# Windowed attention and expert layer: attention by halves of a unit, and a new end of the attention part

## The reference, cut to what matters

```python
def ref(x, w_qkv, w_out, wg, w1, b1, w2, b2):          # x: 4 x 1024 x 256, fp32
    xn = layernorm(x)
    return x + attn(xn, w_qkv, w_out) + ffn(xn, wg, w1, b1, w2, b2)

def attn(x, w_qkv, w_out):                             # 16 heads of 16, blocks of 64 tokens
    q, k, v = split(x @ w_qkv)
    # each block of 64 queries sees its own 64 keys and those of the block before,
    # of these the last 64 up to and with the query itself
    scores = einsum("bhnqd,bhnkd->bhnqk", q_blocks, [k_before, k_own]) / 4
    attn = softmax(where(band_mask, scores, -1e30))
    ob = einsum("bhnqk,bhnkd->bhnqd", attn, [v_before, v_own])
    return ob.reshape(B, L, 256) @ w_out

def ffn(x, ...):       # 8 experts, each token to its best 2, capacity K*N/E, hidden 1024
    ...                # out = sum of gate * y[expert, slot]
```

## Time and profile before

| | |
|---|---|
| median of three runs | 739.16 us (738.99 to 740.17) |
| the profiled execution | 741.44 us |
| its span, first to last instruction | 739.6 us |
| mean granted clock of TensorE | 0.963 |
| PE busy | 687.7 us, 93% |
| DVE busy | 448.9 us, 61% |
| ACT busy | 451.2 us, 61% |
| POOL busy | 379.7 us, 51% |
| the chain that ended last | PE 34% of the span, DVE 2%, issue 1% |

### The profile page before, as it was taken

One profiled execution on the slowest core, in us unless ns is written; L12 is line 12 of the kernel. 1 busy time (PEld: TensorE's weight loads), 2 busy tenths in 40 slices (PEclk: granted clock), 3 DMA queues, 4 the chain that ended last, 5 costly groups with the idle time before them and its releaser, 6 DMA issues. The chain is left out here.

```text
span 739.6 us, 19999 instructions
## 1 busy us (share of the span) xinstructions
PE 687.7 (93%) x6841; PEld 602.1 (81%) x6841; DVE 448.9 (61%) x1679; ACT 451.2 (61%) x1457; POOL 379.7 (51%) x542
## 2 busy tenths in 40 slices
PE   5663899999999999999999998999999999999994
PEld 3453689898898998989989897888888988888874
DVE  7983343543435435344353432798989898998992
ACT  4642570934808438074390741798888888887980
POOL 4646460543605435145251401668666859498772
PEclk9866799999999999999999999899999999999998
DMA  9734131142311422224222003241535343443421
GB/s 306 267 112 146 35 111 55 64 142 85 102 61 64 142 85 89 69 69 135 92 83 73 16 22 106 71 128 53 142 107 156 100 129 105 125 118 97 128 87 67
DMA packets 59224, 76.58 MB, mean 104 GB/s; under 512 B 9488, under 2 KB 51728, under 8 KB 59152
## 3 DMA queue, kind: packets, MB, share of 16 engines
q1 hardware_dynamic: 52656, 58.83, 25.3%
q0 software_dynamic: 6144, 16.79, 7.9%
q10 hardware_dynamic: 352, 0.04, 0.0%
HBM read 51.95 MB, written 17.04 MB: 93 GB/s over the span
## 5 line engine op out<-in xcount | busy, mean ns | idle before, releaser
L1091 ACT ACTIVATE a_p<-a_p,a_nmax 128x128 f32<-128x128 f32 x512 | 198.0, 390 | 34.3 <-DVE a_nmax L1125 33.4
L750 DVE TENSOR_TENSOR m_hl<-m_hf,m_hh 128x512 fp32r<-128x512 f32 x128 | 93.3, 729 | 99.9 <-ACT m_hh L707 99.9
L66 PE MATMUL m_psY<-m_w2h,m_hh 128*128 128x256 f32 x512 | 145.0, 283 | 0.0
L66 PE MATMUL m_psY<-m_w2l,m_hh 128*128 128x256 f32 x512 | 143.9, 281 | 0.0
L66 PE MATMUL m_psY<-m_w2h,m_hl 128*128 128x256 f32 x512 | 143.8, 281 | 0.0
L703 ACT ACTIVATE m_hf<-m_psF,b1T 128x512 f32<-128x512 f32 x128 | 88.3, 690 | 66.2 <-PE m_psF L66 52.0
L1125 DVE CUSTOM_DVE_ANT_0 a_p<-a_psS,mask 128x128 f32<-128x128 f32 x512 | 117.5, 286 | 14.0 <-issue 8.6
L671 POOL CAST m_w2h<-raw 128x256 fp32r<-128x256 f32 x64 | 26.0, 407 | 178.1 <-PE m_psY L66 120.5
L66 PE MATMUL m_psF<-m_xh,w1h 128*128 128x512 f32 x256 | 103.5, 404 | 1.9 <-DVE m_xl L727 1.9
L66 PE MATMUL m_psF<-m_xl,w1h 128*128 128x512 f32 x256 | 102.0, 398 | 0.0
L66 PE MATMUL m_psF<-m_xh,w1l 128*128 128x512 f32 x256 | 102.0, 398 | 0.0
(11 more groups left out here) (193 smaller groups left out, 1364.7 us busy)
## 6 DMA issues: line engine op xcount, KB each, us to landing
raw<-in_L_ffn_w SPq DMA_DIRECT2D x16, 1024.0 KB, 5.5
y_scratch<-y SPq DMA_DIRECT2D x64, 128.0 KB, 1.7
n_xin<-in_L_attn_x SPq DMA_DIRECT2D x8, 512.0 KB, 7.8
xn_scratch<-n_xn SPq DMA_DIRECT2D x8, 512.0 KB, 7.1
a_res<-in_L_attn_x SPq DMA_DIRECT2D x8, 512.0 KB, 4.4
a_rall<-recip_scratch SPq DMA_DIRECT2D x32, 128.0 KB
out<-a_res SPq DMA_DIRECT2D x8, 512.0 KB, 4.3
xnr<-xn_scratch SPq DMA_DIRECT2D x7, 512.0 KB, 5.5
```

The source lines that it names most:

```text
L66: last = pe.matmul(out, a, b, start=(n_start and i == 0), stop=(n_stop and i == n - 1))
L750: dve.tensor_tensor(hl[:, u // HC, u % HC, :], hf[:, u % FR, :], hh[:, u // HC, u % HC, :].bitcast(fp32), ALU.subtract).then_inc(hl_done, 1)
L1091: act.activation(e, e, ACT.Exp, scale=-1.0, bias=nmax[:, r, j:j + 1], accum_out=sums[:, r, j:j + 1]).then_inc(exp_done, 1)
```

## The change

Seven edits, all in the attention phase:

- The second and third group of a unit change places: first both sets of heads for the first four blocks (tiles 0 and 1), then both for the last four. `mt` and `half`, `o_cols`, the band of the mask and the waits of "o" on `o_low` follow.
- On DVE four kinds of waits are left out, each implied by another wait of the same engine: `t_done` before maxima, `rr_in` before the transpose of reciprocals, `pv_done` before the copy to `pT`, and `acc` before the adds of tiles 1 to 3.
- The reciprocals of the last group don't go through DRAM. DVE copies them, each repeated 16 times, into `wide`, which POOL has cleared at the start of the phase (64 partitions by 256 numbers, twice). PE multiplies `wide` by `fold` (two identity matrices added, made at the start by DVE), in four fp32 matmuls of 64 columns into `psR`, a part of a bank of the scores. ACT copies the result to `rall`.
- ACT, and not DVE, copies the transposes of step 126.
- Behind step 127 each engine's work is written out. PE: transposes of step 125, values of group 30, transposes of step 126, the product of tile 0, transposes of step 127, the spreading, the product of tile 1, values of group 31. DVE: copy of step 124, reciprocals, the two copies to `wide`, copy of step 125, multiply of group 30, the last add of unit 6, copy of step 127, adds of tiles 0 and 1, multiply of group 31, adds of tiles 2 and 3.
- The products of tiles 2 and 3 go by halves of the sum: the first halves of both wait for `o_low` of group 30, the second halves for that of group 31.
- The last unit is stored tile by tile, 128 KB each, as soon as each is added.

```diff
         def o_cols(parts, n):
             w, i = n // (STEPS // GRP), n % (STEPS // GRP)
-            return parts[w % 2][:, i // 2, (i % 2) * BLK * WIN:(i % 2 + 1) * BLK * WIN]
+            return parts[w % 2][:, i % 2, (i // 2) * BLK * WIN:(i // 2 + 1) * BLK * WIN]
...
             store(UNITS - 2)
-            spread(GROUPS - 1)
-            store(UNITS - 1)
+            for i in range(O_FIRST, NI):
+                j = ITEMS[i][1]
+                sp.wait_ge(item_free[i % 2], count[UNITS, i] + 1)
+                sp.dma_start(ov[:, LAST_U * UT + j:LAST_U * UT + j + 1, :], res[LAST_U % 2][:, j:j + 1, :])\
+                    .then_inc(res_out[LAST_U % 2], 16)
...
             pool.memset(pad_cols(va[1]), 0.0).then_inc(pads, 1)
+            pool.memset(wide[:, :, :], 0.0).then_inc(zeroed, 1)
...
+            g = ALL - 2
+            act.wait_ge(t_done, g + 1)
+            act.activation(pT[:, g % PTR, :, :].rearrange("p c q -> p (c q)"), psP[g % 2][:, :], ACT.Copy).then_inc(pT_last, 1)
+            act.wait_ge(o_full, LAST_G - 1)
+            act.wait_ge(wide_out, 1)
+            act.activation(rall[LAST_G % 2][:, :], psR[:, :], ACT.Copy).then_inc(rall_last, 1)
...
-                dve.wait_ge(acc, w * K * UT)
+                if j == 0:
+                    dve.wait_ge(acc, w * K * UT)
...
-                    if t >= PR:
-                        dve.wait_ge(t_done, t - PR + 1)
                     alone(dve, s_done, t + 1)
...
-                    if n >= 2:
-                        dve.wait_ge(rr_in[half], 64 * (n // 2))
                     dve.transpose(rrow[half][:, :], rsum[:, :]).then_inc(row_out, 1)
...
                     dve.wait_ge(t_done, g + 1)
-                    if g >= PTR:
-                        dve.wait_ge(pv_done, (g - PTR) // GRP + 1)
...
+            dve.tensor_tensor(fold[:, :], m.eye[:, 0:WIN], m.eye[:, WIN:P], ALU.add).then_inc(fold_done, 1)
...
+            copy(ALL - 4)
+            reciprocals(LAST_G)
+
+            dve.wait_ge(zeroed, 1)
+            for s in range(2):
+                rows = slice(s * WIN, (s + 1) * WIN)
+                each = rsum[rows, LAST_G % 2 * GRP * BLK:(LAST_G % 2 + 1) * GRP * BLK].rearrange("p (c j) -> p j c", j=BLK)
+                dve.tensor_copy(wide[rows, :, :].rearrange("p j (c s d) -> p j c s d", s=2, d=DH)[:, :, :, s, :],
+                                each.unsqueeze(3).broadcast_to([WIN, BLK, GRP, DH])).then_inc(wide_done, 1)
+            copy(ALL - 3)
+            multiply(LAST_G - 1)
+            for w, i, kind, j in ended(ALL):
+                read_item(w, i, kind, j)
+            copy(ALL - 1)
+            for i in range(O_FIRST, O_FIRST + UT // 2):
+                add_out(UNITS, i, ITEMS[i][1])
+            multiply(LAST_G)
+            for i in range(O_FIRST + UT // 2, NI):
                 add_out(UNITS, i, ITEMS[i][1])
...
-                if begins and kind == "o" and j == 0:
-                    pe.wait_ge(o_low, w * (STEPS // GRP))
+                if kind == "o" and (groups or begins and j % (UT // 2) == 0):
+                    pe.wait_ge(o_low, groups or (w - 1) * (STEPS // GRP) + 2 * (j // (UT // 2) + 1))
...
-                mt, half = s // (2 * GRP), s // GRP % 2
+                half, mt = s // (2 * GRP), s // GRP % 2
...
-            for i in range(O_FIRST, O_FIRST + UT):
-                product(UNITS, i, range(3 * KD))
+            turn(ALL - 3)
+            values(LAST_G - 1)
+            turn(ALL - 2)
+            product(UNITS, O_FIRST, range(3 * KD))
+            turn(ALL - 1)
+
+            pe.wait_ge(fold_done, 1)
+            pe.wait_ge(wide_done, 2)
+            for j in range(BLK):
+                ins = pe.matmul(psR[:, j * WIN:(j + 1) * WIN], wide[:, j, :], fold[:, :], start=True, stop=True)
+            ins.then_inc(wide_out, 1)
+            product(UNITS, O_FIRST + 1, range(3 * KD))
+            values(LAST_G)
+            for k in range(KD):
+                for i in range(O_FIRST + UT // 2, NI):
+                    product(UNITS, i, range(3 * k, 3 * k + 3), GROUPS - KD + 1 + k)
```

More of the change, by code:

```diff
@@ L828, in attention_phase @@
     GROUPS = ALL // GRP
+    LAST_U, LAST_G = UNITS - 1, GROUPS - 1
     LAG_I, LAG_Q, LAG_RS, LAG_T, LAG_C, LAG_V, LAG_M, LAG_H = 1, 2, 2, 3, 4, 5, 8, 9
@@ L885, in attention_phase @@
         rall = [sb(f"a_rall{i}", [P, BLK * WIN], fp32) for i in range(2)]
+        wide = sb("a_wide", [P, BLK, P], fp32)
+        fold = sb("a_fold", [P, WIN], fp32)
         pT = sb("a_pT", [P, PTR, BLK, P], fp32)
@@ L894, in attention_phase @@
         bank_of = (0, 1, 0, 2)
+        psR = psS[1][:, 0:BLK * WIN]
         psP = [ps("a_psP0"), ps("a_psP1")]
@@ L908, in attention_phase @@
         q_done = sem("a_q_done")
+        zeroed, fold_done, wide_done, wide_out, pT_last, rall_last = (sem(f"a_{n}") for n in
+            ("zeroed", "fold", "wide", "wide_out", "pT_last", "rall_last"))
         pv_done = sem("a_pv_done")
@@ L997, in _ @@
             store(UNITS - 2)
-            spread(GROUPS - 1)
-            store(UNITS - 1)
+            for i in range(O_FIRST, NI):
[3 more added lines that the diff above has]
+                    .then_inc(res_out[LAST_U % 2], 16)
             for u in range(2):
-                sp.wait_ge(res_out[u], 16 * B)
+                sp.wait_ge(res_out[u], 16 * (B - 1 + (UT if u == LAST_U % 2 else 1)))
         @block.gpsimd
@@ L1081, in read_item @@
                                    ACT.Copy).then_inc(item_free[bank], 1)
-            for t in range(ALL + LAST):
+            for t in range(ALL):
                 for w, i, kind, j in ended(t):
                     read_item(w, i, kind, j)
[L1086 to L1092, removed]
+                r = t % PR
+                for j in range(BLK):
+                    act.wait_ge(max_done, t * BLK + j + 1)
+                    e = pr[:, r, j, :]
+                    act.activation(e, e, ACT.Exp, scale=-1.0, bias=nmax[:, r, j:j + 1],
+                                   accum_out=sums[:, r, j:j + 1]).then_inc(exp_done, 1)
+            g = ALL - 2
[4 more added lines that the diff above has]
+            act.activation(rall[LAST_G % 2][:, :], psR[:, :], ACT.Copy).then_inc(rall_last, 1)
         @block.vector
@@ L1114, in read_item, with maxima @@
                     add_out(w, i, j)
-            dve.memset(rsum[:, :], 1.0).then_inc(rsum_done, 1)
-            for t in range(ALL + LAST):
-                if t < ALL:
-                    r = t % PR
-                    if t >= PR:
-                        dve.wait_ge(t_done, t - PR + 1)
[L1122 to L1128, removed]
+            def maxima(t):
+                r = t % PR
+                alone(dve, s_done, t + 1)
+                for j in range(BLK):
+                    band = 1 if t % (2 * STEPS) < 2 * GRP and j == 0 else 0
+                    dve.tensor_tensor_reduce(
+                        out=pr[:, r, j, :], in0=psS[bank_of[t % 4]][:, j * P:(j + 1) * P],
+                        in1=m.mask[:, band, :], scale=-(DH ** -0.5), scalar=BIG,
+                        op0=ALU.add, op1=ALU.min, accum_out=nmax[:, r, j:j + 1]).then_inc(max_done, 1)
@@ new lines, in multiply, with reciprocals @@
+            def multiply(n):
+                dve.wait_ge(pv_done, n + 1)
+                if n == LAST_G:
+                    dve.wait_ge(rall_last, 1)
+                else:
+                    dve.wait_ge(rall_in[n % 2], 16 * (n // 2 + 1))
+                if n >= 2:
+                    dve.wait_ge(o_low, n - 1)
+                dve.tensor_tensor(of[:, n % 2, :], psO[:, 0:BLK * WIN], rall[n % 2][:, :], ALU.mult).then_inc(o_full, 1)
+            def reciprocals(n):
+                half = n % 2
+                if n == 0:
+                    dve.wait_ge(rsum_done, 1)
+                dve.wait_ge(exp_done, (n + 1) * GRP * BLK)
+                dve.reciprocal(rsum[:, half * GRP * BLK:(half + 1) * GRP * BLK].rearrange("p (c j) -> p c j", j=BLK),
+                               sums[:, half * GRP:(half + 1) * GRP, :]).then_inc(rsum_done, 1)
+                dve.wait_ge(rsum_done, n + 2)
@@ L1129, in _, with copy @@
+            def copy(g):
+                dve.wait_ge(t_done, g + 1)
+                dve.tensor_copy(pT[:, g % PTR, :, :].rearrange("p c q -> p (c q)"), psP[g % 2][:, :])\
+                    .then_inc(pT_done, 1)
+            dve.memset(rsum[:, :], 1.0).then_inc(rsum_done, 1)
+            dve.tensor_tensor(fold[:, :], m.eye[:, 0:WIN], m.eye[:, WIN:P], ALU.add).then_inc(fold_done, 1)
+            for t in range(ALL):
+                maxima(t)
                 n = group_at(t, LAG_M)
                 if n is not None:
-                    dve.wait_ge(pv_done, n + 1)
@@ L1132, in _ @@
-                    dve.wait_ge(rall_in[n % 2], 16 * (n // 2 + 1))
-                    if n >= 2:
-                        dve.wait_ge(o_low, n - 1)
-                    dve.tensor_tensor(of[:, n % 2, :], psO[:, 0:BLK * WIN], rall[n % 2][:, :], ALU.mult)\
-                        .then_inc(o_full, 1)
```

(57 more changed lines are left out.)

## The result

The changed kernel takes 732.93 us, the median of four runs (732.68 to 733.19), against 739.18 (738.99 to 740.17): a ratio of 0.9906, 95% interval 0.989 to 0.9922, 6.25 us less. The direction and the range held. The size did not: 7.97 us were forecast.

The account below looks back on a forecast made before the run. PE bounds mid-attention, and a serial tail of some 14 us the end. Multiply 2.20, products 4.57 and store 1.20 give 7.97 us less: 739.16 to 731.2 us as the median, range 729.6 to 733.6.

Parts of the forecast that it names:

- The halves: Attention, groups 1 and 2 of each unit swapped: 0 for units 0 to 6; last unit's products ready earlier.
- the waits: DVE in attention, four kinds of waits left out: taken as 0, since a met wait is hidden by the instruction ahead.
- rival E: Unit seams in attention: PE waits for rows of q and k, 1.5 us each, giving 741.7 us; chance 0.03.
- One sign of being wrong: End of attention: last exponentials starting later or earlier than 719.56 would show the waits or the order misjudged.
- The start of the last six products: PE's last output products, after group 31's multiply and GpSimd's split: forecast to start at 727.97.
- rival B: Tail on PE: the clock falls to 1.2 GHz, giving 735 to 736 us; chance 0.07.
- From there to the end: Tail from group 31's multiply (726.13) through last six products, add and store: span ends at 731.63 instead of 739.60.
- The prediction's own sign: Last store: more than 2.5 us from the last issue to the end would show the prediction wrong.
- the earlier multiply: Tail, group 31's multiply at 726.13 instead of 728.33: 2.20 us of the gain.
- The 4.57 of the products: Tail on PE, last products shortened from 5.47 to 0.90 us: 4.57 us of the gain.
- the 1.20 of the store: Last store of 128 KB instead of 512: 2.17 us from issue to end instead of 3.37.
- Rival D: Tail: group 31's multiply stays at 728.33, only products and store gain, giving 733.4 us; chance 0.08.

Follow-up runs that it names:

- e9: The changed kernel itself run again, unaltered, as reference on another chip: median 733.82 us, 14.57 us from the multiply of group 29 to the end.
- e2: The changed kernel with the last unit stored by one 512 KB transfer instead of four: median 733.40 us, 14.62 us from the multiply of group 29 to the end.
- e8: The changed kernel with all 24 last output products behind group 31's low part: median 733.41 us, 14.40 us from the multiply of group 29 to the end.
- e7: The changed kernel with tile 1's output product behind group 31's values: median 732.24 us, 13.87 us from the multiply of group 29 to the end.

## Why the prediction was right, and where its size was wrong

- The reading of the bound was right: PE in the middle, a serial tail at the end. The halves and the waits at 0 for units 0 to 6 were right within what can be measured. A stall at the units' seams (rival E) did not appear. One sign of being wrong showed all the same: the last exponential started at 717.19 and not at 719.56. It was a badly chosen sign, as it took an absolute time from one profile. In e9, the same kernel, it is 719.49, and counted from the multiply of group 29 it is 0.65 us in the kernel before and 0.66 in the changed one.
- The start of the last six products was right to 0.1 us (9.12 for 9.06), partly by luck. From the first matmul of the spreading to tile 1's product it was 0.81 (721.04 to 721.85) instead of 0.60, and the value products came 0.24 late; the multiply then followed them 0.08 sooner than taken, and PE the multiply 0.10 sooner (1.74 for 1.84). The two wide copies took 1.03 us instead of 0.66, but end at 719.71, before PE needs them at 721.04. The clock stayed high, as taken (rival B did not occur).
- The term that was mis-sized stands in "From there to the end". It is the last one, the store: "The new store takes 1.7 + 0.47 = 2.17". The landing was right to 0.1 us (1.8 us from the issue, SP went on after 1.9). The prediction's own sign, more than 2.5 us from the last issue to the end, showed: it was about 4.0. The 0.47 us behind the landing were read as something that belongs to the store, while it was what remained when every other engine was already at the barrier. I asked what the store waits for, and not which other engine reaches the end of the block later. The row was in the trace before the change. Put into my own sum it gives: GpSimd's last instruction ended 0.15 before PE's product (730.17 - 730.02), so it would end at 727.97 - 0.15 = 727.82; plus 5.3, plus 0.2 is 733.3, a gain of 6.3 us. Measured: 6.12 in the profiled tail, 6.25 by the medians.
- Of the three parts of the 7.97 us the first, the earlier multiply (2.20), is the one that was paid out, since it moves GpSimd too. The 4.57 of the products and the 1.20 of the store were paid out only down to the drain: e2 shows the split store worth nothing there (+0.05). e8 takes all moved products back and is no slower than the changed kernel (-0.17), and 0.5 us slower than e7. What the 24 products lost in length counted because it brought the store's path below the drain's, not microsecond for microsecond.
- Rival D of the prediction foresaw about the right time (733.4, measured 732.93) for the wrong reason: the multiply was not late. The Trainium skill's rule on DMA (DMA: Bandwidth & Descriptors, Anatomy of one DMA), about 2.0 us fixed, would have given 731.8. The page gives that fit for transfers that GpSimd issues, and this store was issued by SP. The last 128 KB took about 1.9 us until SP went on, between the 2.3 of that rule and the 1.7 of the row. Neither is what the miss came from.

## What to carry to other kernels

When a change shortens the end of a program, list for every engine its last instruction and what its queue still does behind it, not only the chain that ended last: the next bound is whoever had cover. Where GpSimd's queue ends with such a drain, as here, it is best finished some 6 us before the end: hand its last pieces to ACT and DVE. And order the last work by who feeds the slowest finish: here less work ahead of the value products (0.7 us) was worth more than products done early.

## What the runs showed of the hardware

- GpSimd's DRAIN at the end of the attention phase lasted 5.3 us beyond its last instruction in every profile here, after a low part of 0.72 us and after a memset of 0.10 us alike. What it does in that time no run shows.
- It is not so at the end of every phase. In the changed kernel, behind routing (L337) the drain was over at 62.5, 0.1 us after GpSimd's last instruction (59.64 + 2.80), and behind the experts (L582) at 432.5, 5.3 us after it (425.88 + 1.25), where nothing waited for it. GpSimd issued 64 transfers in the experts and 64 in attention, and none in norm and routing. Whether the 5.3 us hang on that no run tests.

```profile
59.64 2.80 POOL L430 TENSOR_SCALAR r_ohV<-r_ohA 128x64 bf16<-128x64 bf16 x6
...
L337 POOLq DRAIN  x1: 2429/2429/2429, 60.1 to 60.1; - x1
...
425.88 1.25 POOL L673 TENSOR_TENSOR m_w2l<-raw,m_w2h 128x256 fp32r<-128x256 f32 x1 [0.18 <-POOL m_w2h L671]
...
L582 POOLq DRAIN  x1: 6461/6461/6461, 426.0 to 426.0; - x1
```

- The two copies of 64 partitions by 256 numbers, whose source is repeated 16 times, did not take the same time. The record of the first is 0.29 us long and that of the second 0.71, and so in each profile looked at. Why was not tried.
- Four fp32 matmuls of 64 columns are eight records, 0.11 us apart (the first two 0.06), and PE went on 0.81 us after the first; the prediction had 0.60, and 0.48 as its other estimate.
